# Position bias of an attention layer: weights split and first logarithms loaded one stage earlier, first bias tiles of attention loaded inside the loop, last copies of the sampling stage rearranged

## The reference, cut to what matters

```python
q   = _gconv1x1(xn, qw)
off = tanh(einsum(gelu(dwconv6x6_stride4(q)), off_pw_w)) * 4      # 8 x 8 sampling points per group
kv  = _grid_sample(xn, vgrid_scaled)                              # at those points
k, v = _gconv1x1(kv, kw), _gconv1x1(kv, vw)
pos  = grid_q[:, :, None, :] - grid_kv[:, None, :, :]             # 1024 queries x 64 keys, per batch and group
bias = sign(pos) * log1p(abs(pos))
bias = relu(bias @ cpb_w1 + cpb_b1)                               # 2 -> 128
bias = relu(bias @ cpb_w2 + cpb_b2)                               # 128 -> 128
bias = bias @ cpb_w3 + cpb_b3                                     # 128 -> 1
attn = softmax(q @ k^T * scale + bias)
out  = attn @ v                                                   # then projection and MLP
```

## Time and profile before

| | |
|---|---|
| median of 3 runs | 4137.58 us (4137.45 to 4138.55) |
| the profiled execution: its own time | 4134.53 us |
| its span, first to last instruction | 4132.6 us |
| mean granted TensorE clock | 0.965 |
| PE busy | 3817.5 us (92%) |
| DVE busy | 2984.4 us (72%) |
| ACT busy | 2600.7 us (63%) |
| POOL busy | 2083.1 us (50%) |

### The profile page before, as it was taken

The page is one execution under the profiler, slowest core; times in us unless marked ns, Lnnn a source line. Parts: engine busy times, 40 slices in busy tenths (PEclk is TensorE's granted clock), DMA queues, the critical chain, the costliest instruction groups (busy, mean ns, idle before and its releaser), DMA issues. The chain is left out here.

```text
span 4132.6 us, 66996 instructions
## 1 busy us (share of the span) xinstructions
PE 3817.5 (92%) x18648; PEld 2414.8 (58%) x18648; DVE 2984.4 (72%) x4512; ACT 2600.7 (63%) x4638; POOL 2083.1 (50%) x1870
## 2 busy tenths in 40 slices
PE   6899999999999999999998999989888747969998
PEld 3555555555555555555555788846676624835555
DVE  7888888888888888888887533364999966245553
ACT  5899999999999999999997433332222342213333
POOL 0555555555555555555554355514776721036664
PEclk8999999999999999999999999999999869989999
DMA  1200000000000000000001200025999952553312
GB/s 49 105 10 10 12 10 10 10 10 10 10 10 10 10 12 10 10 10 10 10 10 38 72 15 1 1 70 219 390 392 400 407 196 64 175 117 72 73 42 82
DMA packets 149909, 327.18 MB, mean 79 GB/s; under 512 B 44600, under 2 KB 49400, under 8 KB 148908
## 3 DMA queue, kind: packets, MB, share of 16 engines
q1 hardware_dynamic: 108332, 174.82, 13.8%
q0 software_dynamic: 41472, 151.01, 9.1%
HBM read 246.50 MB, written 79.04 MB: 79 GB/s over the span
## 5 line engine op out<-in xcount | busy, mean ns | idle before, releaser
L558 POOL TENSOR_TENSOR cpb_sum<-cpb_tab 128x512 f32<-128x512 f32 x1028 | 1045.7, 1048 | 965.2 <-DVE cpb_r L688 964.9
L669 ACT ACTIVATE cpb_h<-cpb_z,net_vec 128x512 f32<-128x512 f32 x1536 | 1006.1, 697 | 50.9 <-PE cpb_z L609 38.3
L606 PE MATMUL cpb_z<-cpb_r,cpb_w2a 128*128 128x512 f32 x2048 | 858.2, 419 | 23.3 <-DVE cpb_h L729 23.3
L688 DVE SCALAR_TENSOR_TENSOR cpb_r<-cpb_sum,cpb_r 128x512 fp32r<-128x512 f32 x1024 | 696.5, 711 | 187.1 <-ACT cpb_r L663 187.1
L607 PE MATMUL cpb_z<-cpb_r,cpb_w2b 128*128 128x512 f32 x2048 | 801.7, 391 | 0.0
L609 PE MATMUL cpb_z<-cpb_r,cpb_w2a 128*128 128x512 f32 x2048 | 799.6, 390 | 0.0
L688 DVE SCALAR_TENSOR_TENSOR cpb_r<-cpb_z,cpb_r 128x512 fp32r<-128x512 f32 x1028 | 662.0, 686 | 159.8 <-ACT cpb_r L663 154.3
L663 ACT ACTIVATE cpb_r<-cpb_z 128x512 fp32r<-128x512 f32 x1028 | 560.4, 604 | 128.2 <-PE cpb_z L593 128.2
L663 ACT ACTIVATE cpb_r<-cpb_sum 128x512 fp32r<-128x512 f32 x1024 | 598.4, 648 | 2.0 <-POOL cpb_sum L558 2.0
L606 PEld LDWEIGHTS cpb_z<-cpb_r,cpb_w2a 128*128 128x128 f32 x2048 | 384.0, 187 | 366.0 <-issue 300.8
L618 PE MATMUL cpb_zo<-cpb_h,cpb_w3w 128*32 128x512 f32 x3584 | 477.3, 605 | 0.0
(11 more groups left out here) (359 smaller groups left out, 5316.5 us busy)
## 6 DMA issues: line engine op xcount, KB each, us to landing
conv_out<-dc_ys SPq DMA_DIRECT2D x576, 64.0 KB, 6.1
cpb_log<-log_dram SPq DMA_DIRECT2D x66, 256.0 KB, 3.2
qk_parts<-gn_r SPq DMA_DIRECT2D x64, 256.0 KB, 2.0
dc_wr<-in_dc_wT SPq DMA_DIRECT2D x9, 1024.0 KB, 5.9
bias_dram<-cpb_bst SPq DMA_DIRECT2D x520, 8.0 KB
net_x<-in_x SPq DMA_DIRECT2D x8, 1024.0 KB, 8.6
sa_qa<-qk_parts SPq DMA_DIRECT2D x16, 512.0 KB
sa_ka<-qk_parts SPq DMA_DIRECT2D x16, 512.0 KB
```

Source lines behind the costliest of these rows:

```text
L558: pool.tensor_tensor(SUM[:, r, :].rearrange("p (y x) -> p y x", x=W), TAB[:, slot, r, 0, :].unsqueeze(1).broadcast_to([P, NF // W, W]), TA ...
L606: pe.matmul(z2[:, bank, :], W2A[:], R1[:, k, :], start=True, stop=False)
L669: act.activation(H2[:, t % 8, :], z2[:, t % 3, :], ACT.Relu, bias=V("cpb_b2")).then_inc(h2a, 1)
L688: v.scalar_tensor_tensor(R2[:, t % RING, :], first_layer(t), 0.0, R1[:, t % RING, :].bitcast(F32), ALU.max, ALU.subtract).then_inc(r2_read ...
```

## The change

1. **Weights.** `W2F` is loaded by SP in the sampling stage. VectorE splits it and fills `W3W` there, between the first two hats and its wait for `pos_ln`. GpSimd clears `W3W` in the sampling stage.
2. **Logarithms.** SP issues the first load of `LOG` in the sampling stage, once all 16 stores of `log_dram` have landed.
3. **GpSimd ahead of the loop.** Spread of half 0, clearing of `H2`, sums, spread of half 1 (before: both spreads, both clearings, sums).
4. **Last copies of sampling.** The copy of the sampled keys (L427) comes before the two masked copies; the two copies into `KBD` go from VectorE to ScalarE, as activations.
5. **Attention's first bias tiles.** SP issues the loads of tiles 0 to 2 in the bias stage, behind the loop and before its wait for the last `staged`, once the stores of all but the last readout have landed. Attention starts with tile 3.

`W2A`, `W2B`, `W3W`, `LOG` and `BS` are now allocated at the right end of SBUF and live through the stages.

```diff
 # layer0_sampling, SP
             sp.dma_start(W1F[:], d["w1rows"]).then_inc(w_in, 16)
+            sp.dma_start(W2F[:], d["cpb_w2"]).then_inc(w2_in, 16)
             sp.wait_ge(pos_step, 6)
...
             sp.wait_ge(log_out, 16 * 16)
+            g["logs"](sp, slice(0, 1))
 # GpSimd
+            pool.memset(W3W[:], 0.0).then_inc(zeroed, 1)
 # ScalarE, behind the last hat
+            act.wait_ge(zeroed, 5)
+            act.wait_ge(k_mm, 1)
+            for gh in range(2):
+                r = slice(gh * DH, gh * DH + DH)
+                act.activation(KBD[r, :, gh * NJ:(gh + 1) * NJ], po[r, :].rearrange("p (a j) -> p a j", j=NJ),
+                               ACT.Copy, scale=DH ** -0.5).then_inc(kbd_ready, 1)
 # VectorE
             hats(0, 1)
+            v.wait_ge(w2_in, 16)
+            v.tensor_copy(W2A[:], W2F[:]).then_inc(split, 1)
+            v.wait_ge(split, 1)
+            v.tensor_tensor(W2D[:], W2F[:], W2A[:].bitcast(F32), ALU.subtract).then_inc(split, 1)
+            v.wait_ge(split, 2)
+            v.tensor_copy(W2B[:], W2D[:]).then_inc(split, 1)
+            v.wait_ge(zeroed, 6)
+            for c in range(8):
+                v.tensor_copy(W3W[:, c, c:c + 1], V("cpb_w3")).then_inc(w3_ready, 1)
             v.wait_ge(pos_ln, 1)
...
+            v.wait_ge(zeroed, 5)
+            v.wait_ge(kv_mm, 1)
+            v.tensor_copy(KV, pk[:]).then_inc(kv_ready, 1)
+
             v.wait_ge(pos_step, n)
             v.tensor_scalar(PX[:], POS[:], V("axis_mask", 0), None, ALU.mult).then_inc(pos_step, 1)
             v.wait_ge(pos_step, n + 1)
             v.tensor_scalar(POS[:], POS[:], V("axis_mask", 1), None, ALU.mult).then_inc(pos_step, 1)
-
-            v.wait_ge(zeroed, 5)
-            v.wait_ge(kv_mm, 1)
-            v.tensor_copy(KV, pk[:]).then_inc(kv_ready, 1)
-            v.wait_ge(k_mm, 1)
-            for gh in range(2):
-                r = slice(gh * DH, gh * DH + DH)
-                v.tensor_scalar(KBD[r, :, gh * NJ:(gh + 1) * NJ], po[r, :].rearrange("p (a j) -> p a j", j=NJ),
-                                DH ** -0.5, None, ALU.mult).then_inc(kbd_ready, 1)
             v.wait_ge(v_mm, 1)
 # layer0_bias, SP
-            logs(slice(0, 1))
-            sp.dma_start(W2F[:], d["cpb_w2"]).then_inc(w_in, 16)
             sp.wait_ge(tables, 2)
-            logs(slice(1, 2))
+            logs(sp, slice(1, 2))
...
+            sp.wait_ge(stored, 16 + 128 * ITERS)
+            for a in range(3):
+                g["load_bias"](sp, a)
             sp.wait_ge(staged, ITERS + 1)
             store(slice(ITERS, ITERS + 1))
 # GpSimd
-            for half in range(2):
-                spread(pool, slice(0, 1), half)
-            pool.memset(W3W[:], 0.0).then_inc(win_zero, 1)
-            pool.memset(H2[:, 4:8, :], 0.0).then_inc(win_zero, 1)
+            spread(pool, slice(0, 1), 0)
+            pool.memset(H2[:, 4:8, :], 0.0).then_inc(h2_zero, 1)
             sums(1, 1)
+            spread(pool, slice(0, 1), 1)
 # TensorE
             pe.wait_ge(split, 3)
-            pe.wait_ge(win_ready, 8)
-            pe.wait_ge(win_zero, 2)
+            pe.wait_ge(w3_ready, 8)
+            pe.wait_ge(h2_zero, 1)
 # VectorE, behind table(0) and table(1): the same lines as added above are taken out
-            v.wait_ge(w_in, 16)
-            v.tensor_copy(W2A[:], W2F[:]).then_inc(split, 1)
...
-                v.tensor_copy(W3W[:, c, c:c + 1], V("cpb_w3")).then_inc(win_ready, 1)
 # layer0_attention, SP
-            for a in range(PAIRS):
-                if a >= 3:
-                    sp.wait_ge(sim_mm, a - 2)
-                sp.dma_start(BS[:, a % 3, :], g["bias"].rearrange("(a p) n -> a p n", p=P)[a]).then_inc(bias_in[a % 3], 16)
+            for a in range(3, PAIRS):
+                sp.wait_ge(sim_mm, a - 2)
+                g["load_bias"](sp, a)
                 if a == 4:
                     g["prefetch_w2"](sp, w2_in)
```

More of the change, by code:

```diff
@@ L125, in layer0_sampling @@
                                                        s.sem("pos_sgn"), s.sem("w1_step"))
+        W2F, W2D = s.sb("w2f", [P, P]), s.sb("w2d", [P, P])
+        W2A, W2B, W3W = g["W2A"], g["W2B"], g["W3W"]
+        split, w3_ready, w2_in = g["split"], g["w3_ready"], s.sem("w2_in")
         block = s.block()
@@ L452, in layer0_bias @@
         TPI = KPI * 2
-        W2F = s.sb("w2f", [P, P])
-        W2A, W2B = s.sb("w2a", [P, P], F32R), s.sb("w2b", [P, P], F32R)
-        W3W = s.sb("w3w", [P, 8, 32])
+        W2A, W2B, W3W = g["W2A"], g["W2B"], g["W3W"]
         EXP = s.sb("exp", [P, 2, NF], BF16)
@@ L459, in layer0_bias @@
         SUM = s.sb("sum", [P, 4, NF])
-        LOG, TAB = s.sb("log", [P, 2, 4, 2, W]), s.sb("tab", [P, 2, 4, 2, W])
+        LOG, TAB = g["LOG"], s.sb("tab", [P, 2, 4, 2, W])
         H2 = s.sb("h2", [P, 8, NF])
         BST = s.sb("bst", [P, NF])
-        W2D = BST[:, 0:P]
         z1 = s.ps("z1", [P, 4, NF])
@@ L466, in layer0_bias @@
         zo = s.ps("zo", [P, NF])
-        w_in, split, win_zero, win_ready = s.sem("w_in"), s.sem("split"), s.sem("win_zero"), s.sem("win_ready")
+        split, w3_ready, h2_zero = g["split"], g["w3_ready"], s.sem("h2_zero")
         exp_ready = s.sem("exp_ready")
@@ L472, in layer0_bias @@
         h2_free = s.sem("h2_free")
-        log_in, table_step, tables, sum_ready = s.sem("log_in"), s.sem("table_step"), s.sem("tables"), s.sem("sum_ready")
+        log_in, logs = g["log_in"], g["logs"]
+        table_step, tables, sum_ready = s.sem("table_step"), s.sem("tables"), s.sem("sum_ready")
         staged = s.sem("bias_staged")
@@ L542, in _ @@
                 sp.wait_ge(tables, i * 2 + 4)
-                logs(bass.ds((i + 2) % ITERS, 1))
+                logs(sp, bass.ds((i + 2) % ITERS, 1))
+            sp.wait_ge(stored, 16 + 128 * ITERS)
+            for a in range(3):
+                g["load_bias"](sp, a)
             sp.wait_ge(staged, ITERS + 1)
@@ L705, in _ @@
             table(1)
-            v.wait_ge(w_in, 16)
-            v.tensor_copy(W2A[:], W2F[:]).then_inc(split, 1)
-            v.wait_ge(split, 1)
-            v.tensor_tensor(W2D, W2F[:], W2A[:].bitcast(F32), ALU.subtract).then_inc(split, 1)
-            v.wait_ge(split, 2)
-            v.tensor_copy(W2B[:], W2D).then_inc(split, 1)
-            v.wait_ge(win_zero, 2)
-            for c in range(8):
-                v.tensor_copy(W3W[:, c, c:c + 1], V("cpb_w3")).then_inc(win_ready, 1)
             v.sem_inc(h2v, FREE)
@@ L743, in layer0_attention @@
         qf, af = Q[:].rearrange("p t n -> p (t n)"), AO[:].rearrange("p t n -> p (t n)")
-        BS = s.sb("bs", [P, 3, HW])
+        BS, bias_in = g["BS"], g["bias_in"]
         E = s.sb("e", [P, 3, NC * 2, NJ])
@@ L750, in layer0_attention @@
         pv = s.ps("pv", [P, 2, NF])
-        bias_in = [s.sem(f"bias_in{u}") for u in range(3)]
         sim_mm, maxed, shifted, exp_done = s.sem("sim_mm"), s.sem("maxed"), s.sem("shifted"), s.sem("exp_done")
@@ L2597, in build @@
             g["log_dram"] = nc.dram_tensor("log_dram", (GROUPS * B * NJ // KPI, 2, 4, 2, W), F32).ap()
+            g["W2A"], g["W2B"] = k.sb("w2a", [P, P], F32R, side="right"), k.sb("w2b", [P, P], F32R, side="right")
+            g["W3W"] = k.sb("w3w", [P, 8, 32], side="right")
+            g["LOG"] = k.sb("log", [P, 2, 4, 2, W], side="right")
+            g["log_in"], g["w3_ready"], g["split"] = k.sem("log_in"), k.sem("w3_ready"), k.sem("split")
+            g["logs"] = lambda sp, i: sp.dma_start(
+                g["LOG"][:], g["log_dram"][i].rearrange("o s r a x -> o (s r a x)").broadcast_to([P, 2 * 4 * 2 * W])
+                .rearrange("p (s r a x) -> p s r a x", s=2, r=4, a=2)).then_inc(g["log_in"], 16)
             layer0_sampling(nc, d, g)
+            g["BS"] = k.sb("bs", [P, 3, HW], side="right")
+            g["bias_in"] = [k.sem(f"bias_in{u}") for u in range(3)]
+            g["load_bias"] = lambda sp, a: sp.dma_start(
+                g["BS"][:, a % 3, :], g["bias"].rearrange("(a p) n -> a p n", p=P)[a]).then_inc(g["bias_in"][a % 3], 16)
             g["WO"], g["W1"] = a.sb("wo", [P, CT, C]), a.sb("w1", [P, CT, HID])
```

3 lines of the change are left out of this document (removed).

## The result

The changed kernel is slower: 4150.62 us (4149.08 to 4155.06, 7 runs) against 4137.92 (4136.48 to 4139.53, 7 runs) on the same chip, a ratio of 1.0031 [95%: 1.0021 to 1.0040]. The forecast was 4127.1 us. The profiled execution took 4150.62 us around a span of 4148.8.

A forecast was written before the change was run, and what follows sets the result against it. The prediction took the loop to be bound by TensorE, with only its edges to win: 7.0 us at the loop's start plus 3.5 at attention's make 10.5, so 4137.58 - 10.5 = 4127.1 us, range 4124.0 to 4131.2.

The forecast's parts named there:

- The split is hidden: Sampling stage: VectorE's added 1.3 to 3.8 us fit its 5.7 us wait for ScalarE, cost 0; rival that they don't, 0.03.
- The first logarithms early: Sampling's end: LOG's load comes some ten us ahead of the bias stage, where VectorE had idled 3.41 us; cost 0.
- The key copy, 1.0: Sampling's end: key copy at about 98.3 instead of 99.30, all behind it 1.0 us sooner; bounds 0.6 and 1.2.
- KBD on ScalarE: Sampling's end: the two KBD copies, moved from VectorE, end at 103.9 at the latest, before the value copies at 104.4.
- The table operations beside GpSimd: Bias stage's start: VectorE's four table operations meet GpSimd's spread, clearing and sums; first residual at 110.5, 0.2 us taken off.
- VectorE late: Loop's start: residuals of tiles 4 to 7 wait for GpSimd, 2.1 us less gain, 4129.2 us; chance 0.09.
- The second seam, 3.5: Bias stage to attention: early bias tile loads let TensorE start at 2255.35 rather than 2258.85, 3.5 us gained; bounds 0 and 3.6.
- clock stays up: Attention's start: TensorE still at 2.4 GHz when it starts 3.5 us sooner, 13.0 us gained in all, 4124.6; chance 0.06.
- The readouts still 33.25 apart: Bias stage's loop: a sign of being right, each of the 64 iterations still takes 33.25 us.
- weights and columns into sampling: Sampling stage: VectorE's moved casts, subtraction and column copies take 1.3 us, upper end 3.8, in its idle time; cost 0.
- the loop's rhythm changes: Bias stage's loop: moved tiles and another engine phase slow iterations; at 0.35 us each, 11.9 slower, 4149.5 us; chance 0.05.

The follow-up runs named there:

- all_aligned: Changed kernel with 32 empty bytes at the very right end of SBUF, ahead of KBD, so every right-hand tile moves; 4141.30 us, ratio 1.0011.
- w_right_416: Changed kernel with 416 empty bytes ahead of W2A, the weights still at the right end of SBUF; 4128.61 us, ratio 0.9983.
- w_aligned: Changed kernel with 32 empty bytes ahead of W2A, moving W2A, W2B, W3W, LOG and BS 32 bytes down; 4145.43 us, ratio 1.0016.
- before_all_off32: Kernel before the change with 32 empty bytes ahead of W2F, so weights and residuals move together; 4137.05 us, ratio 1.0001.
- w_left: Changed kernel with W2A and W2B in one tile at SBUF's left end, ahead of R, later overlaid by the MLP's zeros; 4126.86 us, ratio 0.9979.

## Why the prediction was wrong

- **The split is hidden**: right. 1.3 us at 71.3 to 72.6, taken out of a wait of 5.7.
- **The first logarithms early**: right. They are issued at 91.53, and VectorE's 3.41 us of waiting is gone.
- **The key copy, 1.0**: right. It follows the matmuls by 0.11 us instead of 1.15. It didn't come at the forecast 98.3, since the sums' matmuls ended 1.69 us late in this execution (99.84 against 98.15). What the prediction didn't have is the clock: the stretch from the key copy to the stage's end was 1.51 us shorter, since TensorE's granted clock was 1.00 in the key and value matmuls. Together 1.04 + 1.51 - 1.69 = 0.86, the amount by which sampling ends sooner. Neither the lag nor the clock belongs to the change. With the new sampling code the key copy starts between 98.53 (all_aligned) and 100.64 (w_right_416), and the clock is 1.00 in six of eight traces but 0.50 in w_aligned and all_aligned, whose stretch takes 6.32 us instead of 4.58. With the old code it is 0.50 in four of nine traces (6.09 to 6.17 us), the kernel before among them, and at or near 1.00 in the two us behind the key copy in the other five (5.09 to 5.34 us), though TensorE had been idle for as long. In before_all_off32, for one:

```profile
101.45 1.16 PE L233 MATMUL smp_po<-smp_off,smp_kw 128*128 128x128 f32 x8 [1.89 <-DVE smp_off L427]
```

  That the trace of the kernel before has the low level and that of the kernel after the high one is luck, and the forecast's agreement at sampling's end (104.53 for 104.4) comes of the lag and the clock cancelling. With the low level in both, the change gains 1.04 - (6.32 - 6.09) = 0.8 us here, inside the 0.6 to 1.2 of the prediction. KBD on ScalarE ends at 103.17, ahead of the last value copy, as reckoned.
- **The table operations beside GpSimd**: right in kind. The first two took 2.92 and 1.88 us, each ending within 0.15 us of the end of GpSimd's clearing (107.70), and the loop's first matmul came at 109.71, inside the 109.5 to 109.9 of the forecast. The next four residuals, which read two tiles in SBUF, took 3.71 us beside GpSimd where the first four took 2.48, but TensorE didn't wait for them. The rival "VectorE late" did not come: the first readout was at 115.85 for a forecast 115.6.
- **The second seam, 3.5**: right. It is 3.5 in the kernel after, 3.9 in the pair that differs in nothing else. The stores weren't delayed, and "clock stays up" didn't come: the granted clock is 0.50 (1.2 GHz) from 2270 to 2272 in the kernel after, and it was so already from 2268 on, while TensorE was idle.
- **The readouts still 33.25 apart**: wrong, and this is the step that failed. Under "weights and columns into sampling" the prediction priced the moved instructions and gave the new place of the tiles no price; the rival "the loop's rhythm changes" named it ("W2A, W2B, W3W and LOG lie elsewhere in SBUF") and put it aside with "its instructions are the same, and the mean iteration equals the first one". The instructions are the same; they take 3.5 ns longer each, 6144 times. The second reason was about the loop before and could say nothing about a loop with other addresses. That rival's arithmetic was near (0.35 us an iteration, 4149.5 us; measured 0.34 and 4150.62), though its 0.35 was an example and not worked out from anything. Its chance of 0.05 had no more behind it than such reasons. Of its two mechanisms the runs keep the place (of W2A and W2B, not of W3W) and drop the phase.

The forecast gain is there and is overlaid: with the weights put in step with R (both starts equal modulo 256) and all else as in the change, the kernel takes 4126.86 us, 9.3 less than before for a forecast 10.5. This w_left is the version to keep: 0.9979 [0.9970, 0.9988] of before and faster than the kernel after.

Shown is the dependence: on the difference of the two starts, fast at 0 and 256 bytes, slow at 64, 128, 160 and 224 modulo 256. Not settled is why; that R2 alone costs 0.22 of the 0.29 us isn't explained by each matmul paying for itself. Other differences modulo 256 (32, 96, 192) weren't tried, nor other kinds of operands but the third layer's. Open too are some 4 us between the medians of kernels whose loops agree or nearly do (w_aligned and all_aligned, w_left and best).
